# Normalised rows made one unit further ahead, in three buffers, in the projections of a two-layer triangle kernel

## The reference, cut to what matters

```python
def _L0_conv_ref(z, mask, ln_in_w, ln_in_b, w_ap, b_ap, w_ag, b_ag, w_bp, b_bp, w_bg, b_bg, ...):
    m = mask[..., None]
    zn = _layer_norm(z, ln_in_w, ln_in_b)
    a = m * jax.nn.sigmoid(zn @ w_ag + b_ag) * (zn @ w_ap + b_ap)
    b = m * jax.nn.sigmoid(zn @ w_bg + b_bg) * (zn @ w_bp + b_bp)
    p = jnp.einsum('bikc,bjkc->bijc', a, b)
    x = _layer_norm(p, ln_out_w, ln_out_b) @ w_z + b_z
    g = jax.nn.sigmoid(zn @ w_g + b_g)
    return x * g
...
x = x + _L0_conv_ref(_ln_c(x), ...)
t = t + _L0_ffn_ref(_ln_t(t), ...)
x = x + _L1_conv_ref(_ln_c(x), ...)
t = t + _L1_ffn_ref(_ln_t(t), ...)
```

## Time and profile before

| what | value |
|---|---|
| median of 3 runs | 1974.67 us (1967.63 to 1975.97) |
| profiled execution | 1967.55 us, its span 1965.7 us |
| mean granted clock of PE | 0.951 of full speed |
| PE busy | 1592.1 us, 81% |
| DVE busy | 1416.6 us, 72% |
| ACT busy | 1221.1 us, 62% |
| POOL busy | 1009.9 us, 51% |
| HBM traffic over the span | 172 GB/s |

### The profile page before, as it was taken

The page is one execution under the profiler, slowest core; times in us unless marked ns, Lnnn a source line. Parts: engine busy times, 40 slices in busy tenths (PEclk is TensorE's granted clock), DMA queues, the critical chain, the costliest instruction groups (busy, mean ns, idle before and its releaser), DMA issues. The chain is left out here.

```text
span 1965.7 us, 38544 instructions
## 1 busy us (share of the span) xinstructions
PE 1592.1 (81%) x10716; PEld 1057.0 (54%) x10716; DVE 1416.6 (72%) x4747; ACT 1221.1 (62%) x2982; POOL 1009.9 (51%) x1722
## 2 busy tenths in 40 slices
PE   4777774989786989968888858997857999999997
PEld 2443342978674558835555527886745444444442
DVE  5777773046697978868888840366955999999986
ACT  4777773633385989937777754432856666666641
POOL 4776771025586840036676640145765666666642
PEclk9999997999998989979999988999975999999999
DMA  3567555468897537037788754589976666666652
GB/s 107 161 166 188 161 157 136 140 184 291 275 362 244 163 111 314 1 101 207 211 225 230 221 140 142 151 285 299 319 245 159 186 180 185 183 186 180 177 145 81
DMA packets 387914, 373.42 MB, mean 190 GB/s; under 512 B 155040, under 2 KB 303264, under 8 KB 385696
## 3 DMA queue, kind: packets, MB, share of 16 engines
q1 hardware_dynamic: 342688, 304.32, 53.1%
q10 hardware_dynamic: 45056, 67.13, 9.9%
HBM read 186.80 MB, written 150.99 MB: 172 GB/s over the span
## 5 line engine op out<-in xcount | busy, mean ns | idle before, releaser
L474 ACT ACTIVATE cp_sig<-cp_pv 128x384 f32<-128x384 f32 x512 | 243.1, 490 | 149.6 <-PE cp_pv L525 147.2
L1534 DVE TENSOR_TENSOR ex_xe<-ex_spread,ex_xd 128x512 f32<-128x512 f32 x512 | 317.6, 683 | 21.4 <-PE ex_spread L1785 18.4
L1801 PE MATMUL ex_po<-ex_xe,ex_expert 128*64 128x512 f32 x1024 | 251.0, 612 | 0.0
L454 ACT ACTIVATE cp_xn<-cp_x,cp_lift,cp_rstd 128x64 f32<-128x64 f32 x512 | 196.2, 439 | 34.7 <-POOL cp_lift L402 34.7
L1656 ACT ACTIVATE ex_xn<-ex_x,ex_lift,ex_rstd 128x64 f32<-128x64 f32 x512 | 182.0, 429 | 21.0 <-POOL ex_lift L1578 21.0
L429 POOL TENSOR_TENSOR cp_b_stage<-cp_b_stage,cp_mask 128x256 f32<-128x256 f32 x256 | 151.7, 613 | 84.2 <-DVE cp_b_stage L353 67.3
L525 PE MATMUL cp_pv<-cp_weight,cp_zt 64*128 64x320 f32 x1024 | 174.4, 457 | 22.2 <-DVE cp_b_stage L353 21.3
L351 DVE SCALAR_TENSOR_TENSOR a_res<-cp_pv,cp_mask,cp_sig 128x64 f32<-128x64 f32 x512 | 132.6, 323 | 77.8 <-ACT cp_sig L474 74.5
L508 PE MATMUL cp_tp<-ident,cp_xn 128*128 128x128 f32 x512 | 85.8, 291 | 123.2 <-ACT cp_xn L454 123.2
L525 PE MATMUL cp_pv<-conv_weight,cp_zt 64*128 64x320 f32 x1024 | 174.2, 458 | 2.3 <-DVE cp_b_stage L353 2.1
L814 POOL TENSOR_TENSOR cc_p<-cc_p,cc_room 128x512 f32<-128x512 f32 x64 | 104.5, 1633 | 138.7 <-DVE cc_room L783 138.2
(11 more groups left out here) (211 smaller groups left out, 3716.9 us busy)
## 6 DMA issues: line engine op xcount, KB each, us to landing
gate_scratch<-cp_sig SPq DMA_DIRECT2D x128, 256.0 KB, 2.5
b_scratch<-cp_b_stage SPq DMA_DIRECT2D x128, 256.0 KB, 3.8
cc_room<-b_scratch SPq DMA_DIRECT2D x128, 256.0 KB, 2.8
ex_xd<-ex_xt SPq DMA_DIRECT2D x256, 128.0 KB, 2.6
cp_x<-in_x SPq DMA_DIRECT2D x64, 256.0 KB, 3.3
cc_room<-gate_scratch ACTq DMA_DIRECT2D x64, 256.0 KB, 4.0
cc_p<-in_x SPq DMA_DIRECT2D x64, 256.0 KB, 4.2
after_conv<-cc_p ACTq DMA_DIRECT2D x64, 256.0 KB, 3.7
```

What stands on the lines that cost most here:

```text
L454: ins = act.activation(xn[u.mod(2)][:, i, 0, :], xs[u.mod(8)][:, 0, i, :], ACT.Identity, scale=rstd[q][:, k, i * H:i * H + 1], bias=lift[q ...
L474: act.activation(sig[u.mod(2)][:, :, :, i, :].rearrange("p k h c -> p h k c"), pv[slot(u, i)][:, :, 0:3 * C].rearrange("p h (k c) -> p h k ...
L1534: dve.tensor_tensor(xe[u.mod(2)][:, :, h, i * P:(i + 1) * P], pb[k][:].rearrange("p (e t) -> p e t", e=EP), xd[u.mod(8)][:, h, i * P:(i + ...
L1801: ins = pe.matmul(po[h * HALF:(h + 1) * HALF, :], expert[:, e, :], xe[u.mod(2)][:, e, h, :], start=e == 0, stop=e == EP - 1)
```

## The change

The order inside a step stays. Normalising is done for unit s + 3 in place of s + 2, with three buffers `xn`, and all that comes before it moves by one unit too: the load, the sums of the second call, the measures, the guess and the refining. `flip`, `take`, `project`, `gates` and `product` stay where they are. Where a unit's own number decides (the guess and the refining, each four units), the step that does it moves by one, so that a unit's work is done one step earlier throughout.

```diff
-        xn = [m.sb(f"xn{q}", [P, R, H, C]) for q in range(2)]
+        xn = [m.sb(f"xn{q}", [P, R, H, C]) for q in range(3)]
-        FIRST, LAST = -10, G + 4
+        FIRST, LAST = -11, G + 4
 # SP
                     store_gate(s - 1)
-                    load(s + 9)
+                    load(s + 10)
                     store_b(s - 1)
-                    store_sum(s + 7)
+                    store_sum(s + 8)
 # DVE
-                    add_y(s + 8)
-                    measure(s + 8)
+                    add_y(s + 9)
+                    measure(s + 9)
...
-                    if s.mod(4) == 3:
-                        first_guess(s + 5)
+                    if s.mod(4) == 2:
+                        first_guess(s + 6)
 # POOL, and ACT alike
-                    if (u - 2).real:
-                        pool.wait_ge(xt_made, u.n - 1)
+                    if (u - 3).real:
+                        pool.wait_ge(xt_made, u.n - 2)
...
-                    normalise(s + 2)
+                    normalise(s + 3)
+                    if s.mod(4) == 3:
+                        refine(s + 5, 0)
                     if s.mod(4) == 0:
-                        refine(s + 4, 0)
-                    if s.mod(4) == 1:
-                        refine(s + 3, 1)
+                        refine(s + 4, 1)
 # ACT
-                    normalise(s + 2, 0)
+                    normalise(s + 3, 0)
                     gates(s, 2)
                     gates(s, 3)
-                    normalise(s + 2, 1)
+                    normalise(s + 3, 1)
 # PE
-                    turn_y(s + 8)
+                    turn_y(s + 9)
```

More of the change, by code:

```diff
@@ L409, in normalise @@
                     q, k = (u.base // 4) % 2, u.mod(4)
-                    to = xn[u.mod(2)][:, :, 1, :]
+                    to = xn[u.mod(3)][:, :, 1, :]
                     def column(t):
@@ L450, in normalise @@
                         act.wait_ge(refined, u.div(4) * REFINES + REFINES)
-                        if (u - 2).real:
-                            act.wait_ge(xt_made, u.n - 1)
+                        if (u - 3).real:
+                            act.wait_ge(xt_made, u.n - 2)
                     for i in range(part * R // 2, (part + 1) * R // 2):
-                        ins = act.activation(xn[u.mod(2)][:, i, 0, :], xs[u.mod(8)][:, 0, i, :], ACT.Identity,
+                        ins = act.activation(xn[u.mod(3)][:, i, 0, :], xs[u.mod(8)][:, 0, i, :], ACT.Identity,
                                              scale=rstd[q][:, k, i * H:i * H + 1], bias=lift[q][:, k, i * H:i * H + 1])
@@ L507, in flip @@
                     for i in range(R):
-                        ins = pe.transpose(tp[:, i * P:(i + 1) * P], xn[u.mod(2)][:, i].rearrange("p h c -> p (h c)"),
+                        ins = pe.transpose(tp[:, i * P:(i + 1) * P], xn[u.mod(3)][:, i].rearrange("p h c -> p (h c)"),
                                            ident[:])
```

## The result

The changed kernel takes **1889.37 us** (median of 4 runs, 1888.85 to 1899.14), the kernel before 1972.06 (4 runs, 1967.63 to 1975.97). The ratio is 0.9584, with a 95% interval of 0.956 to 0.9609: 4.2% faster. The forecast was 1896 us, the range 1881 to 1922. The profiled execution has a span of 1887.1 us, against 1965.7 before: 78.6 us less.

A forecast was written before the change was run, and what follows sets the result against it. Prediction: no engine is full; a ring of mutual waits between engines bounds each unit. Gains of 48.8 and 26.4 us less 3 for the starts make 72 us off 1967.55, so 1896 us; range 1881 to 1922.

The forecast's parts named there:

- The ring that was cut: Flip and ACT's gates wait for each other once per unit: 4.56 us in the first call, 4.73 in the second.
- First call: Ring through project's three bank pairs decides: 3.76 us per unit, 0.80 less over 61 intervals, 48.8 us gained.
- Second call: Same ring with add_y and measure on DVE: 4.36 us per unit; 52 x 0.37 + 9 x 0.80 = 26.4 us gained.
- The starts: At each call's start one more unit is normalised, added and measured first: 3 us lost for both calls.
- Transfers: DMA in units that store b: debt of 1.2 or 1.5 us covered by time gates have to land; cost nothing.
- The rival of the transfers: Units storing b run at 4.06 and 4.73 us, giving back 19 us, so 1915 us; chance 0.26.
- the rule that the prediction cites from the Trainium skill: Transfers below 512 bytes miss line rate, so units storing b would stay as slow as their stores.
- PE's clock: Rival: PE's granted clock falls to its lower level and PE becomes the bound, 220 us more, 2188; chance 0.02.
- Signs that were worded too strictly: Sign of being right: PE's waits in project end with DVE's product in every unit.
- the one ring that binds: After the change, gate 1 to gate 2, product 2, project 1, gate 1: 3.76 us; via DVE in second call 4.36.

The follow-up runs named there:

- e1: Kernel before with only the third buffer of normalised rows, old order kept: ratio 1.0001.
- e2: Changed kernel with two buffers of normalised rows in place of three, new order kept: ratio 0.9656.
- e11: Changed kernel with a block's eight transfers of b sent over seven units in place of four: 1891.04 us.
- e8: Changed kernel with ACT's first normalising part between gates 2 and 3 and DVE's measure between products 2 and 3: 1885.85 us.
- e3: Kernel before with three buffers and only ACT's normalising one unit further ahead; loads, sums, measures, guess and refining stay: 1963.91 us.
- e4: Changed kernel with both parts of ACT's normalising behind gates 2 and 3: 1907.67 us.
- e7: Changed kernel with ACT's first normalising part moved between gates 2 and 3: 1889.27 us.
- e5: Changed kernel with DVE's measure moved from behind the sum to behind product 3: 1893.2 us.
- e6: Changed kernel with the edits of both e4 and e5: 1900.5 us.

## Why the prediction was right

- **The ring that was cut.** The flip's waits for ACT fell from 63 to one. That the order does it, with the buffer as a condition for the last part, is shown by e1 (1.0001) and e2 (0.9656). The prediction did not separate the two; its sentence that "the third buffer costs no time" is right, but alone it also gains none.
- **First call.** Forecast 3.76 us per unit and 48.8 us; measured 3.72 and 51.4. The path is the one that was walked. Two of its pieces, product to project and project to gate, came out at 0.82 and 0.85 where the earlier trace rows gave 0.83 and 0.88.
- **Second call.** Forecast 4.36 and 26.4; measured 4.30 in a unit and 27.9 in all. Again the path is right and the handovers are shorter (0.80 and 0.85).
- **The starts.** Costed at 3 us, the upper end. They cost nothing in this execution: the flip of unit 2 came 0.2 us earlier in the first call, and 0.8 us earlier behind the first flip in the second. With the two terms above, 2.6 + 1.5 + 3, this is about what the forecast was too high by (6.6 us); the single microseconds elsewhere nearly cancel. Part of the closeness is luck: the sum starts from an execution of 1967.55 us, and the median of the kernel before is 1972.06. Between the medians lie 82.7 us, where the terms give 72.
- **Transfers.** Costed at nothing in the units that store b: right, shown by e11, and by flips at 150.66, 154.37, 158.09 and 161.88 us, in units that store b, with none near 4.06. In the whole first call one unit from unit 2 on took 4.02 us and the others at most 3.91; in the second none took more than 4.36. The rival of the transfers, 0.26, is out for this change. The debt is there: from 150 to 166 us, where b is stored, a gate took 3.6 us to land, where the median of both calls of the kernel before was 2.5. It was covered, as forecast, but for 1.2 us that gates of the first call waited, in four times. By the rule that the prediction cites from the Trainium skill ("DMA: Bandwidth & Descriptors", Specifications) the units would have stayed as slow as b's stores; they did not. At units of 3.92 us in the second call the cover is gone, and the rival's mechanism is what e8 shows.
- **PE's clock.** 1.00 in both stretches, so this rival is out. e3 shows that its mechanism exists in this kernel, behind pauses of PE of 1.4 to 2.5 us; in the changed kernel's stretches PE's waits for other engines were never above 0.6 us in the first call and 0.4 in the second.
- **Signs that were worded too strictly.** In the first call the profile names DVE as what ended project's wait in 21 units, not in every one; in the second in 57. The arithmetic of the timeline, and e4 and e7, which make the longest gap longer and shorter and get units of 3.89 and 3.56, carry the ring there.
- **What the prediction lacked** was the rule behind its ring. It had the one ring that binds and not the other three beside it, which made no error here, but made e4, e5 and e6 miss.

## What to carry to other kernels

Where two engines wait for each other once per pass, walk the ring in the timeline and cut it by order, then walk the next one. With three buffers used in turn and four uses per pass, as here, it is the handover time plus the longest gap between neighbouring uses, so work in a gap is to be spread and not only moved. Move everything that feeds the moved step with it (e3), and give it the buffer that keeps the first engine of the step from waiting (e2). When a unit has become shorter, look at bursts of transfers before their mean share: spreading the same bytes was worth 13 us here.

## What the runs showed of the hardware that was not expected

A wait of one engine for another can cost PE's clock as well, and the same pause does not always do so. In the first call of e3 PE paused fourteen times for 2.49 to 2.50 us. After three of these pauses the granted clock stayed at 1.00, after eleven it fell (0.59 over the 4.2 us from 123.80). There one pause cost twice, about 2.5 us and then 1.1 us in sixteen matmuls. In its second call the clock fell after two of thirteen pauses of 1.4 to 1.5 us, and in e8 after one of 1.92 us, in the unit of 6.4 (0.73 from 980 to 985 us). Pauses of 0.86 to 0.94 us in each unit of the kernel before left it at 1.00. What else decides beside the length of a pause, these runs do not show. And PE's busy time per unit is not its need: it rose from 3.3 us to 211.8 / 60.6 = 3.5 in the first call (225.5 / 3.72 = 60.6 units), with the same matmuls, although the engine did no more.
